# Output projection of batches 0 to 6 by seven products of half-size blocks, in a fused attention kernel on one core

## What is computed

```python
scale, shift = split(emb @ W_emb + b_emb)
xn  = rms_norm(x, g_norm) * (1 + scale) + shift
q, k, v = heads(xn @ W_qkv)                      # 16 heads of 64
q, k = rms_norm(q, g_q), rms_norm(k, g_k)
o = softmax(q @ k.T * 64 ** -0.5) @ v            # 512 x 1024
out = x + o + o @ W_out                          # the last product is what changes
```

## Time and profile before

| | |
|---|---|
| median of 3 runs | 2210.16 us (2209.71 to 2211.5) |
| profiled execution | 2209.7 us, span 2207.9 us |
| mean granted TensorE clock | 0.996 |
| busy share PE / PEld | 98% / 90% |
| busy share DVE / ACT / POOL | 74% / 68% / 41% |
| DMA | 497.5 MB, mean 225 GB/s, 63.5% of 16 engines |

### The profile page before, as it was taken

One profiled execution on the slowest core, in us unless ns is written; L12 is line 12 of the kernel. 1 busy time (PEld: TensorE's weight loads), 2 busy tenths in 40 slices (PEclk: granted clock), 3 DMA queues, 4 the chain that ended last, 5 costly groups with the idle time before them and its releaser, 6 DMA issues.

```text
span 2207.9 us, 39088 instructions
## 1 busy us (share of the span) xinstructions
PE 2158.0 (98%) x13392; PEld 1983.1 (90%) x13392; DVE 1623.6 (74%) x2999; ACT 1492.5 (68%) x3205; POOL 908.0 (41%) x1241
## 2 busy tenths in 40 slices
PE   7789899999999999999999999999999999999999
PEld 3778789999999999999999999999999999999988
DVE  4799987669856788567875688656886669856676
ACT  4688976568755787467864688645876468755664
POOL 3876653435422454224632254332552235422430
PEclk9999999999999999999999999999999999999999
DMA  8676466786656864667656665477655676656752
GB/s 320 243 281 257 163 220 229 247 290 226 207 191 218 299 209 170 241 219 263 206 189 236 238 247 200 160 260 278 216 202 173 242 281 224 204 192 229 266 184 96
DMA packets 141525, 497.53 MB, mean 225 GB/s; under 512 B 14864, under 2 KB 61968, under 8 KB 140304
## 3 DMA queue, kind: packets, MB, share of 16 engines
q1 hardware_dynamic: 141328, 495.03, 63.5%
HBM read 425.77 MB, written 69.21 MB: 224 GB/s over the span
## 4 chain that ended last, share of the span: by engine, by line
PE 78%; ACT 6%; DVE 4%; issue 3%; POOL 1%; DMA 1%; ACTq 0%; SPq 0%; DVEq 0%; POOLq 0%
PE proj_bank L611 17%; PE proj_bank L613 17%; PE proj_bank L612 16%; PE flip_bank L736 8%; PE score_bank L727 5%; PE score_bank L728 4%; PE pv_bank L747 4%; PE pv_bank L748 4%; ACT k_hi L860 2%; PE score_bank L700 2%; PE flip_bank L707 1%; ACT probs L875 1%; DVE k_lo L1058 1%; DVE stage L986 1%; ACT pt_hi L885 1%
## 5 line engine op out<-in xcount | busy, mean ns | idle before, releaser
L611 PE MATMUL proj_bank<-w_ring,xa_hi 128*128 128x384 f32 x1792 | 626.4, 350 | 12.3 <-POOL xa_lo L1198 7.1
L613 PE MATMUL proj_bank<-w_ring,xa_lo 128*128 128x384 f32 x1792 | 605.4, 338 | 0.0
L612 PE MATMUL proj_bank<-w_ring,xa_hi 128*128 128x384 f32 x1792 | 604.5, 337 | 0.0
L875 ACT ACTIVATE probs<-score_bank,neg_max 128x512 f32<-128x512 f32 x512 | 352.8, 691 | 202.1 <-DVE neg_max L1088 168.4
L1099 DVE TENSOR_TENSOR pt_lo<-flip_bank,pt_hi 128x512 fp32r<-128x512 f32 x512 | 347.9, 685 | 173.1 <-ACT pt_hi L885 170.0
L885 ACT CAST pt_hi<-flip_bank 128x512 fp32r<-128x512 f32 x512 | 296.9, 588 | 230.5 <-PE flip_bank L736 170.0
L1088 DVE TENSOR_REDUCE neg_max<-score_bank 128x1 f32<-128x512 f32 x512 | 345.9, 685 | 82.4 <-PE score_bank L728 78.8
L611 PEld LDWEIGHTS proj_bank<-w_ring,xa_hi 128*128 128x128 f32 x1792 | 338.9, 189 | 37.1 <-issue 8.7
L612 PEld LDWEIGHTS proj_bank<-w_ring,xa_hi 128*128 128x128 f32 x1792 | 339.4, 189 | 11.4
L613 PEld LDWEIGHTS proj_bank<-w_ring,xa_lo 128*128 128x128 f32 x1792 | 338.2, 189 | 0.0
L1191 POOL TENSOR_TENSOR v_split<-stage,v_split 128x256 fp32r<-128x256 f32 x128 | 94.5, 740 | 512.0 <-ACT v_split L848 511.8
(11 more groups left out here) (92 smaller groups left out, 3808.9 us busy)
## 6 DMA issues: line engine op xcount, KB each, us to landing
w_ring<-qkv_store SPq DMA_DIRECT2D x392, 768.0 KB, 5.6
w_ring<-wo_store SPq DMA_DIRECT2D x108, 512.0 KB, 4.6
qkv_store<-w_ring SPq DMA_DIRECT2D x56, 768.0 KB, 6.4
x_tile<-in_x SPq DMA_DIRECT2D x36, 512.0 KB, 6.7
w_raw<-in_x SPq DMA_DIRECT2D x112, 128.0 KB, 5.2
out<-w_raw SPq DMA_DIRECT2D x112, 128.0 KB, 4.7
w_raw<-in_w_qkv SPq DMA_DIRECT2D x16, 768.0 KB, 8.2
wo_store<-w_ring SPq DMA_DIRECT2D x16, 512.0 KB, 5.4
```

The lines of the kernel that those rows point to most:

```text
L611: nc.tensor.matmul(dst, a_hi, w[:, 0, :], start=start, stop=False, skip_group_check=shared)
L612: nc.tensor.matmul(dst, a_hi, w[:, 1, :], start=False, stop=False, skip_group_check=shared)
L613: return nc.tensor.matmul(dst, a_lo, w[:, 0, :], start=False, stop=stop, skip_group_check=shared)
L875: nc.scalar.activation(probs[h][:, i, :], score_bank[n % 2][:, :], ACT.Exp, bias=neg_max[:, n:n + 1], accum_out=row_sum[:, n:n + 1]).then_ ...
```

## The change

P of batches 0 to 6 becomes one job by the same seven products: 28 steps `P<n>` of 6 matmuls with 512 columns (n = 4j + 2i + half as in C), with 14 weight units of 1 MB that take 4 chunks of the ring. P of batch 7 stays the plain product. `JOB_TURN = "0 P 1 2 3"`.

- **Weights**: eight forms (W11, W21, W12, W22 and four sums; W_out with the identity added), prepared in batch 0. 16 raw tiles of 128 x 512 (`G`), 8 `I` additions of the identity in 4 steps, 16 DVE sums `J` (128 x 512), 32 splits `L` (ACT the high parts, DVE and POOL 16 low parts each), 32 stores `H` of 512 KB. A split works in one of four slots in `o_lo`, which is free only when the store four before has landed. All `L` steps stand in `HEAD`, ahead of the first P, and P has no fresh units any more.
- **Activations**: `O1` of DVE now writes o in full into `o_sum` (which lies over `o_hi`). `Z` steps of batches 0 to 6: DVE makes 8 block sums (128 x 512), ACT rounds 14 forms, POOL subtracts 14. Forms use the four slots in `o_lo`. `Q` steps are left for batch 7 alone.
- **Evictions**: ACT keeps the first product (`U0`, `U1`: 128 x 512 from PSUM), DVE has 12 `R` steps of 128 x 512 instead of 16 of 128 x 256, POOL adds a shared sum to three residual tiles per row tile (6 `U` steps of 128 x 512). Residual tiles are 8 of 256 KB, in a ring of six; SP loads and stores 8 of each per batch instead of 16 of 128 KB.
- **Orders**: all lists are new, and the cut between `HEAD`, `BODY` and `TAIL` lies later: `BODY` starts with `0C17`, and P of the batch before (`-P`) follows `0C27`.

```diff
-JOB_TURN = "0 P0 P1 1 P2 P3 2 3".split()
+JOB_TURN = "0 P 1 2 3".split()
 HEAD = { "TensorE":
...
+        6C21 6C22 5F5 5W3 5W4 5F6 6C23 6C24 5W5 5F7 6T0 6C25 6T1 6C26 5W6 6C27 5W7 8C0 8C1 6S0 8C2 6S1 6S2 8C3
+        6S3 8C4 6S4 8C5 6S5 8C6 8C7 6S6 6F0 6S7 6F1 8C8 6W0 6F2 8C9 6F3 6W1 7T0 8C10 7T1 6F4 8C11 6F5 6W2 6W3
+        7S0 6F6 6W4 6W5 6F7 7S1 6W6 6W7 7S2 7S3 8C12 8C13 8C14 7S4 8C15 7S5 7F0 7S6 7W0 7S7 7F1 7F2 7F3 7W1 7W2
+        7F4 8C16""".split(),
     "ScalarE":
...
+        6O0 6F4 7V0 6F5 L5 L6 8D0 6F6 6F7 L7 7S0 7V1 7S1 7S2 L8 7S3 L9 L10 6O1 L11 7N3 L12 L13 L14 7S4 +Y6 7S5
+        L15 +Y13 7F0 L16 L17 L18 7F1 L19 L20 7S6 8D1 L21 7S7 L22 7F2 L23 L24 L25 7N7 L26 L27 7F3 L28 7F4 L29 L30
+        L31 Z0 Z1""".split(),
     "VectorE":
...
+        J8 J9 L19 7S7 J10 J11 8D1 L21 L23 7U1 8E6 7F1 7N4 7N5 I3 L25 7F2 J12 J13 J14 L27 7N6 J15 L29 7F3 L31 6O1
+        8E7""".split(),
     "SyncE":
...
+        G0 G1 8W2 G2 G3 G4 G5 8W3 8W4 8W5 8W6 8W7 8W8 H0 H1 H2 8W9 8W10 H3 H4 H5 H6 G6 G7 H7 G8 G9 8W11 8W12 H8
+        H9 H10 H11 H12 H13 H14 G10 G11 H15 G12 G13 H16 H17 H18 H19 H20 H21 H22 G14 G15 H23 H24 H25 H26 H27 H28
+        H29 H30 H31 E0 E1 E2 E3 E4 E5""".split(),
 BODY = { "TensorE":
+        0C17 0C18 -1W3 0C19 -1F5 0C20 0C21 -1F6 -1W4 0C22 0C23 -1W5 -1F7 -1W6 0C24 0C25 0T0 0T1 0C26 0C27 -P0
+        -P1 -P2 -1W7 0S0 0S1 -P3 0S2 -P4 -P5 -P6 0S3 0S4 -P7 0S5 -P8 0S6 0S7 -P9 -P10 0F0 -P11 0F1 -P12 0W0 0W1
...
     "ScalarE":
+        -1O0 -1F5 0D2 -1F6 0D3 -1F7 1D0 0T0 1D1 0T1 -U0 1D2 -1O1 -Z2 0S0 -U1 -Z3 0S1 0V0 -Z4 0S2 -Z5 0V1 0S3 -Z6
...
     "VectorE":
+        0E8 0E9 -1F4 -1O0 0D2 0E10 -1F5 0D3 -1F6 0E11 0E12 1D0 -1F7 0E13 0T0 0T1 -1O1 0S0 1D1 -Z0 -Z1 0S1 -Z2
...
     "SyncE":
+        0W13 -W0 -W1 -W2 -W3 -W4 -W5 -O0 -W6 -E6 -W7 -O1 -W8 -E7 -W9 +X0 -W10 +X1 -W11 -W12 -W13 2W0 2W1 2W2 2W3
...
+OUT_FORMS = 8
+OUT_TURN = [0, 1, 3, 6, 7, 4, 5]
...
-        n = 3 if unit[0][0] == "C" else 2
+        n = unit_width(unit[0]) // P
...
+            def out_product(job, n):
+                j, i, half = n // 4, n // 2 % 2, n % 2
+                unit, u = (job, 2 * j + half), 2 * j + i
+                dst = proj_bank[i][:, :]
+                if half == 0:
+                    if j == 1:
+                        pe.wait_ge(proj_copied, COPIED[job] + i + 1)
+                    else:
+                        pe.wait_ge(proj_drained, DRAINED[job] + (i - 1 if j == 0 else 2 * (j - 2) + i + 1))
+                    pe.wait_ge(form_lo, job[1] * 2 * PRODUCTS + u + 1)
...
+            def round_form(b, u):
+                j, i = divmod(u, 2)
+                if j in (0, 1, 6):
+                    pairs_there(act, b, PAIRS // 2 - 1 if j == 0 else PAIRS - 1)
+                else:
+                    act.wait_ge(form_summed, b * 8 + {3: 0, 2: 2, 4: 4, 5: 6}[j] + i + 1)
+                if u >= 4:
+                    act.wait_ge(proj_done, TILES[("P", b, 0)] + u - 4 + 1)
...
+                nc.scalar.copy(form(u, 0), o_block(*FORM_IN[j], i)).then_inc(form_hi, 1)
+            def split_out_hi(n):
+                r, f = divmod(n, OUT_FORMS)
+                out_factor_there(act, r, f)
+                if n >= 4:
+                    m = C_SPLITS + n - 4
+                    act.wait_ge(w_stored[m % 8], 16 * (m // 8 + 1))
...
+                nc.scalar.copy(out_split(n)[0], out_raw(r, OUT_BLOCK[f])).then_inc(wo_hi_done, 1)
...
+            def store_out_split(u):
+                r, f = divmod(u, OUT_FORMS)
+                out_lo_wait(sp, u)
+                n = C_SPLITS + u
+                at = u % 4 * 2
+                sp.dma_start(wo_store[f, r // 2, :, r % 2, :, :], f32(o_lo[:, at:at + 2, :])).then_inc(w_stored[n % 8], 16)
```

772 lines of the change are left out of this document (468 added, 304 removed).

## The result

The changed kernel is slower: 2231.1 us, median of four runs (2227.1 to 2237.3), against 2209.9 for the kernel before on the same chip. The ratio is 1.0097, with a 95% interval of 1.0072 to 1.0122. The profiled execution is the 2237.3, with a span of 2235.5; against the profiled execution before (2209.7) it is 27.6 us longer. It is the slowest of the four: by the medians the loss is 21.2 us, and where the other 6 went in the faster executions no trace shows.

What follows compares the result with a forecast made beforehand. TensorE's matmul distances were taken to bound the middle batches, DVE and steps chained to it batch 0. From 2209.7, minus 49 for P, plus 15 for waits and 28 for batch 0, gave 2203.7, 2204 for the median; range 2183 to 2226.

Steps and rivals of the forecast that it cites:

- What P saves: P in seven batches: 168 matmuls of 512 columns replace 384 of 256, saving 7.0 us a batch, 49 in all.
- Rival D: P: a 512-column matmul costs as much as two of 256, 240 ns, saving 5.8 a batch; 2212 us; chance 0.05.
- The ring: P's weight units in seven batches: odd units land slightly late for TensorE, charged 1.1 us a batch (bounds 0.3 and 4).
- The 2.1 us a batch: Batches with the new P: unhidden latency at the last pair and the weight ring together, 15 us in seven.
- The last pair's chain: Start of P, at `-P4`: ACT, DVE and POOL steps after W7 end late, charged 1.0 us a batch (bounds 0 and 2).
- As throughput it is hidden: Batches 1 to 7 beside P: added DVE 7.4, ACT 4.9 and POOL 15.9 us a batch cost nothing as throughput.
- rival B: P and C behind it: six odd units 0.8 us late starve TensorE, 3 us a batch, 21 in all; 2225; chance 0.15.
- Batch 0: Stretch before the first P: DVE's added W_out work ends it at 354.2, first P at 368.4; charged 28 us.
- Rival A: Batch 0: the store chain through slots bounds, 2.2 us a store, 16 us more, first P after 385; about 2220; chance 0.20.
- The clock: Batch 0 ahead of the first P: TensorE perhaps with stretches at the lower clock, no size given.
- Batch 7: P of batch 7: its units come as 1 KB pieces, with 7 us and more to land, at no cost.

Runs made afterwards that it cites:

- e9: e4 with POOL's added low parts of the forms and residual sums cut to 32 and 8 columns instead of 512: 2216.7 us.
- e4: The changed kernel with only the first half of each W unit of P loaded in batches 0 to 6: 2236.9 us.
- e16: e4 with POOL's low parts of the forms and sums into the residual each made in two operations of 256 columns: 2229.0 us.
- e2: The changed kernel with eight DVE reductions of about 1.1 us added ahead of diagonal steps 1 to 3: 2232.9 us.
- e1: The changed kernel without the ten raw W_out tile loads of preparation rounds 1 to 3: 2227.3 us.
- e3: The changed kernel with three slots for the W_out splits instead of four: 2243.1 us.
- e13: The changed kernel with raw W_out tiles loaded early and new queue orders from `6S0` to the end of batch 1: 2224.5 us.
- e5: e4 without DVE's eight form sums of a batch: 2218.0 us.

## Why the prediction was wrong

**What P saves: right.** From start to start a 512-column matmul of P takes 226 ns (230 to 234 were forecast), ten of them in 2.26 us of the changed kernel's trace:

```profile
692.80 0.39 PE L687 MATMUL proj_bank<-w_ring,o_lo 128*128 128x512 f32 x1
...
695.06 0.39 PE L688 MATMUL proj_bank<-w_ring,o_lo 128*128 128x512 f32 x1
```

Adding up the distances of all matmuls by kind (each to the next one's start, so that a wait counts to the matmul ahead of it; four batches, us in a batch):

```
                     C      P   transposes  scores  pv     sum
before           120.6   46.8      33.2      31.2   32.3   264.1
changed          122.0   40.9      34.9      32.7   31.8   262.4
e9               122.3   39.8      32.8      32.2   31.6   258.8
```

Without ring waits in P (e9) P takes 39.8 us, 7.0 less than before. The exact match with the sum's 7.0 is in part luck: a wait of 0.8 us ahead of `0S2`, which belongs to the next term, is in the 39.8, and P's matmuls alone saved 7.8. Rival D is out. The ring's waits of the changed kernel stand largely under transposes, since a transpose comes just ahead of them.

**The 2.1 us a batch: mis-sized.** The step named two places. The last pair's chain costs 0.7 to 0.8 us in each batch, close to the 1.0 charged, but not at `-P4`, which never waits for POOL's `o_lo`. A little ahead of it `0S2` waits for the exponential of `0S0`, and that stands in ACT's queue behind `-1O1` and `-Z2`. The ring costs about 1.5 us a batch in P (10.3 us in seven batches) and 0.7 in the C units behind P (4.6 us; before had 1.0), 2.1 together, where 1.1 was charged. Not all the odd units are a little late, as the sum had it: all five waits behind those 10.3 us, 1.0 to 3.4 us long, are at `P13`, for unit 7 alone. A P unit lands in 4.7 us at least and 4.9 in the median, where 5.0 at least was charged, but unit 7 took 6.7 to 8.7 us in the five batches that waited and 5.2 and 5.4 in the two that didn't; why was not taken apart. The two kinds of waits, each in one batch:

```profile
654.52 0.50 PE L808 MATMUL score_bank<-k_hi,q_split 128*128 128x512 f32 x1 [0.66 <-ACT probs L995]
...
937.67 0.80 PE L687 MATMUL proj_bank<-w_ring,o_lo 128*128 128x512 f32 x1 [3.41 <-DMA w_ring<-wo_store]
```

What was left out is DVE beside POOL. "As throughput it is hidden: (191.6 + 7.4)/257 is 77% of DVE" is the sentence that failed. It priced the sums at 0.741, a group's mean in the kernel before, and let POOL's 15.9 us a batch cost nothing because POOL has room. In P's stretch both meet: the sums take 0.93 us on the mean in the changed kernel, up to 1.80, since they and the scaling steps take turns with POOL (e4, e16). That is why e4, which took away the ring's waits, won nothing. Another 1.7 us a batch is in C and the scores of the table (e9 against before, less P's 7.0). About 0.9 of it is the wait for C's units behind P (3.9 us in the four batches of e9, 0.4 in those of before), the second half of rival B's mechanism; the rest, in small pieces, no run took apart. So the batches came to 261.8, just short of rival B's mark ("a batch over 262"). B named the ring in P and in C and nearly had the size of the loss; it had nothing of DVE and POOL.

**Batch 0: the step that failed at the root.** "If every idle moment is filled it ends at 350.4; with the same 3.8 idle as before at 354.2" took DVE for the engine that ends the stretch, because it had been busy 90% in batch 0 of the kernel before. The prediction said that it would be wrong at its root if this wasn't so, and e2 shows that it isn't: DVE was busy 56% there, and 9.6 us more work in its waits cost nothing. The edit put 32 splits in a chain in which every engine waits for the next, behind loads that wait for the chain; that a queue has room says nothing of such a chain. The sum should have been made round by round: load, diagonal step, then eight splits and four sums that take turns. The rounds took 14.3 and 19.4 us without the load (e1) and 17.4 and 20.8 with it. Three rounds of 17.4 from the diagonal step `I1` (319.1) are 52 us, and with the prediction's own 14.2 us of TensorE's steps behind them the first P comes near 385. This is an estimate from rounds measured afterwards; the trace of before has the lengths of the single steps (0.62, 0.72, 1.32 us, and a landing), but whether they add up to such a round was not worked out.
Rival A, the one on the slower side, named 2.2 us a store and the first P after 385, and both came about: 20 splits in 47 us are 2.35 each. Its mechanism, the slots' round, isn't the one in that stretch: ACT waited 1.4 us for slots, against 15.5 for the diagonal step behind the loads. It is near, though: with three slots it costs 10.7 us (e3), and with the loads early and the orders new it is ACT's longest wait there, 9.8 us (e13). It is the next limit of this preparation.

**The clock was charged nothing.** The 45.3 us at the first P are not all waits. TensorE's waits from 285 us on grew by 39.6, `6S0` came 4.7 us earlier than before (the early part of the new orders is better), and 10.4 are left. From 319 to 366 the granted clock is 0.54, and 0.80 from 366 to 387, where before it was 1.00: TensorE had idled three quarters of the time. Score matmuls of 512 columns start 0.42 us apart there (342.11 to 342.53, 342.53 to 342.96) instead of 0.23:

```profile
342.11 0.63 PE L808 MATMUL score_bank<-k_hi,q_split 128*128 128x512 f32 x1
...
342.53 0.63 PE L809 MATMUL score_bank<-k_lo,q_split 128*128 128x512 f32 x1
...
342.96 1.91 PE L817 MATMUL flip_bank<-ident,probs 128*128 128x128 f32 x8
```

By these distances, as an estimate, the 12 us of work in the first stretch would have been about 6 at the higher of the two levels (2.4 GHz against 1.2), and, by its 0.80, the 20 us of the second stretch about 4 shorter: 10 together. The prediction wrote "perhaps with stretches at the lower clock" and put no number to it. The Trainium skill (TensorE: Matmul & The Clock Gate, "What's actually happening") says that the lower clock is the default and that activity lifts it. By that rule the trace agrees: 0.54 where TensorE is 25% busy, 0.80 in the 21 us behind.

**Batch 7.** The prediction gave its units "7 us and more to land, at no cost". They landed in 3.7 to 8.5 us, 5.3 in the median, and one of them cost 0.8 us.

**The range and the chances.** 2183 to 2226 left the result out by 5 us. The two accounts erred the same way and were treated as apart; A and B each had the right size, and both together, 2220 + 21 of B's, were never added. Slower was given 0.29.

## What to carry to other kernels

When work is moved to a place ahead of its consumer, don't price it by the engine that is busiest on the mean; write down one round of the chain it forms (load, first step, turns between the engines, release) and multiply, and ask what stands behind each waiting step in the same queue. When two waits lie at one place, taking away one shows nothing until the other is gone too: e4 alone would have said that nothing is to be won in P's stretch, and e5 and e9 say otherwise. And work given to an engine with room isn't free if another engine has to take turns with it: look at the longest operation of a group and not only at its mean, and at what ends just ahead of its end on the other engine.

## What the runs showed of the hardware

DVE's operations between SBUF tiles and POOL's take turns. In the changed kernel 38 of the 384 scaling steps last over 0.52 us (0.48 alone, 1.53 the longest), and all 38 end 281 to 286 ns behind the end of an operation of POOL's. Of the 56 form sums 25 began under one of POOL's `Z` or `U`, and all 25 end 545 to 554 ns behind it, up to 1.80 long. Steps with an operand in PSUM don't take part: with POOL busy for more than half of their time or not, `pt_lo` takes 0.684 and 0.686, `neg_max` 0.686 and 0.684, the evictions 0.55. Nor does every operation of POOL shut DVE out: of 16 scaling steps begun under `qk_rstd` (1.01 us long, on 4 columns) none was longer, and nine of them had over half a microsecond of it still ahead. Which of two waiting steps goes next isn't fixed, either. One `stage` of POOL's (197.68) took 2.48 us instead of 0.61, while three scaling steps begun after it went ahead; and in e16 one scaling step (1993.84) took 2.23 us, through three operations of POOL's in a row, and ended 284 ns behind the last. The kernel before shows the same turns, scaling steps up to 1.51 us; it was there to be read, in the longest of the group.
The Trainium skill (SBUF — State Buffer, "SBUF: two separate sides") has this as an exclusive lock on a pair of ports that VectorE shares with GpSimd: whichever starts first keeps the pair for its whole instruction and the other blocks. Where DVE's steps are long, the trace agrees in all 63 cases. Under `qk_rstd` nothing was blocked, in nine cases that could have shown it, so the rule is too wide; and in the `stage` of 2.48 us the operation whose record starts first isn't the one that went first.
